# Softmax normalisation moved behind the value product in two of four attentions, with a new order of all engines' steps

## Chip, cores and metric

One core of a Trainium2 chip. The time is device microseconds of one execution; lower is better. The engines are called PE (TensorE), DVE (VectorE), ACT (ScalarE), POOL (GpSimd) and SP (the DMA queue).

## The reference

A chain of four cross attentions, a state-space layer and an MLP over x (4 batches x 1024 rows x 256, fp32); each attention has 77 keys per batch. What matters here are the third (L2) and the fourth (L3) attention, 16 heads of 16 elements each:

```
q = heads(x @ Wq + bq)                      # 16 heads of 16
s = q @ k.T / sqrt(16)                      # 77 keys, masked
p = softmax(s)                              # L2: masked again, divided by (sum + 1e-9)
o = concat over heads of p @ v              # 1024 x 256
x = x + o @ Wo + bo                         # then a layer norm
```

The second attention (L1) has 16 heads of 64, the first (L0) 8 heads of 32.

## The kernel before

**Tiling.** The 4096 rows are 32 tiles of 128 rows. Four lanes each work through 8 tiles, in two phases. The first phase (about 24 to 240 us) does L0 and the input of the state-space scan, the scan follows (to about 330 us), and the second phase does L1, L2, L3 and the MLP, for the first two batches until about 830 us and for the last two from about 890 us. Tables of keys and values are made between. Each lane owns two PSUM banks, `bank(lane, 0)` and `bank(lane, 1)`; the tiles `pr`, `front` (its part `pr2`), `big`, `zt` (the name `z` in the code), `tt` (`t`), `mx` and `rec` have one slice per lane.

**Order.** Each lane's steps stand in a list (`attention_steps`, `lane_steps`). Which lane's next step an engine takes is written out by hand, one character per step, in the strings `TURNS`, one for each engine. An engine issues its steps in this order and each step waits for semaphores, so a step that is not ready holds all that stands behind it on its engine.

**An attention of L2 or L3, in two groups of 8 heads** (`.0` in `pr`, `.1` in `front`): PE makes scores (L861), DVE adds or bounds by the mask into SBUF (L1369, L1372) and takes the row maximum (L1379), POOL subtracts (`below`, L1642), ACT takes the exponential (L1189). In L2, POOL multiplies by the mask (`maskmul`, L1628). DVE sums each head's 77 probabilities (`rowsum`, L1390), in L2 adds 1e-9 (`den_eps`, L1398), and takes 8 reciprocals per row (`recip`, L1405). The 128x616 probabilities are multiplied by them: in L2 by DVE (`weigh`, L1410), in L3 by POOL (`scale`, L1647). Then PE turns them in five 128-column pieces (`pturn`, L876), ACT and DVE copy the pieces back (`pturn_main`, L1193; `pturn_rest`, L1415), and after both groups PE multiplies by the values (`mix`, L911), with output transposed: 128 channels x 128 rows, twice. ACT copies that to SBUF (`mixed`, L1197), PE projects it (`proj`, L925) and DVE adds it to x (`resid`, L1432). L1 goes the same way with `shift` (L1385) for `below`, with `weigh`, and with no `mixed` and `proj` (its `mix` is L904). Layer norms are `stats` (L1344), `aggr` (L1348), POOL's `rstd` (L1603) and `norm` (L1357), turned by PE (`turn`, L800) and copied by ACT (L1165, L1168). POOL adds bias rows to x (`prebias`, L1616). The MLP is L961, L1213 and L972.

Of the kernel before, what the change touches and what calls it, by code (L numbers as in the profile page):

```python
# [9 lines left out]
ALU = mybir.AluOpType  # L10
# [3 lines left out]
P = 128  # L14
# [49 lines left out]
WEIGHED = (L1, L2)  # L64
# [19 lines left out]
def attention_steps(a):  # L84
# [7 lines left out]
    norm = ["rowsum"] + ["den_eps"] * (a is L2) + ["recip", "weigh" if a in WEIGHED else "scale"]  # L92
# [4 lines left out]
    steps += [(s, second) for s in masked + norm + turns] + [("mix", a.name)]  # L97
    return steps + ([] if a is L1 else [("mixed", a.name), ("proj", a.name)]) + [("resid", a.name)]
# [82 lines left out]
def setup_steps():  # L181
# [7 lines left out]
    "tensor": ("item_mm", "turn", "query", "scores", "pturn", "mix", "proj", "uproj", "ssm", "fc1", "fc2",  # L189
               "w2_mm", "wqt_mm", "k_mm", "wk_mm", "vt_mm", "vwo_mm", "v_mm", "scan_mm", "gap_turn", "more_pe"),  # L190
    "scalar": ("item_act", "turned", "query_bias", "expo", "pturn_main", "mixed", "u_sb", "gelu", "w2_sb", "wqt_sb", "k1_sb", "vt_sb", "silu", "more_act"),
    "vector": ("ctx_stats", "ctx_norm", "item_dve", "stats", "aggr", "norm", "bound", "rowmax", "shift", "rowsum", "den_eps", "recip", "weigh",
               "pturn_rest", "heads", "resid", "resume", "wk_sb", "vwo_sb", "k_sb", "v_sb", "carry", "ends", "gap", "agree"),
    "gpsimd": ("ctx_rstd", "head_masks", "row_masks", "value_zero", "zeros", "rstd", "prebias", "keep", "below", "maskmul", "scale", "gain", "offset", "masks", "fold", "vtw_zero"),
# [3 lines left out]
def lane_steps(lane):  # L198
# [12 lines left out]
    for n, run in enumerate(second):  # L211
# [19 lines left out]
        "iiiiiiii01iiiiii0iiiiiiiiiii2ii1ii230132030103132012301202103211022301321203023123021230130130032031022110101202"  # L231
        "3103212130132102013012032120132031231033012301300210302311230130321022031230132310012013201213210130230132212323"
        "1010323002103211230132130201302102332013321230030120323011012312203321203123121323231032123aa0a3aaaasaaasaasasas"
        "asaasaasaasaasaasaasaasaasaasasaasaasaasaasaasaasasasaasasasaasaasasasaaasaaaasaa0132010103123020102001010121130"
        "2100021232020130101303230301013102100002020s12011012232102111011013203030210212333213222102212013101032313203030"
        "3203312321021213203020131010030003213201320121313013212021211013032103032012023132322310221210310202313130120303"
        "3023312323120121032020131010031002303201323230131210212110132011032301312020231320322123212012032010213130301032"
        "03333231210132120302013102100300312321322131313bb2121212113bbbbb2b3bb3bb2bb3bbbb2bbbbbbbb3bbbbbb32b3bbbbbbbbbbb3"
        "bb2bbbb210221020102301002301030102130121031010333302103020210212102030312013010310030232130232103131202121102130"
        "1103203031021202313232213221021031010232313020310332330213231032101020230210013100032132102303121310131111203120"  # L240
        "2323102301202023132032213221201201301013231302030332031323231021210230201310100300123032123023103131202121120111"
        "0230320301312021302323123212201031201013231302030332330123210231212030203110130031232132323131012221321032332121"
        "32332322323332313333"),
    "vector": (
        "i0110ii013ii22i3i2iiiiiii3i0012103300123101101323330002221201101322213233200312021002012023322111213200003330322"
        "1133210101000131322301020110112221011013031222232003233301100333130223011110002001131311223220032332223033330200"
# [36 lines left out]
        "20222311113122232331322022233333233333132"),  # L283
    "sync": (
        "aaaaa2aaa0aa20a1aa3a3aaaaaa1aaaaaa102a0a13232aa020113a31a0102aa20330a1120323011a22330110322a3aa130212032a00b1aa1"
        "3312020111322300233b0bb13011012220bb2333001013301222213032302113"),
}

# [1417 lines left out]
```

## Time and profile before

| what | value |
|---|---|
| three runs | 1394.56, 1398.53, 1402.86 us (median 1398.53) |
| profiled execution | 1401.9 us, span 1400.1 us |
| mean granted TensorE clock | 0.98; 1.00 from 440 to 1280 us |
| PE busy | 1278.1 us (91%), 9411 matmuls |
| DVE busy | 1047.8 us (75%), 2236 instructions |
| ACT busy | 677.4 us (48%), 1503 instructions |
| POOL busy | 654.1 us (47%), 760 instructions |
| HBM | 23.26 MB read, 8.39 MB written |

The profile is of one execution. An instruction's duration runs from its start to the end of its writes, so a following one on the same engine may start before it ends; busy time counts each moment once. "Idle before, releaser" is the time in which an engine stood before an instruction, and the instruction that ended it. The chain is followed back from the last instruction, at each step to what released it.

### The profile page before, as it was taken

The numbers are of one execution on the slowest core, as the hardware profiler recorded it, in microseconds if no ns is written. First come the engines' busy times: TensorE is split into PE (matmuls) and PEld (weight loads), VectorE is DVE, ScalarE is ACT, GpSimd is POOL, SyncE is SP. The second block draws the span as 40 slices with busy tenths as digits, with TensorE's granted clock in tenths as the row PEclk, the third lists the DMA queues.
The fourth block names the chain that finished last, engine by engine and source line by source line (L and its number), as shares of the span: only waits on it lengthen the run. The fifth ranks groups of instructions, "written<-read, shape, count | busy, mean of one in ns | idle before, by whom it ended". The sixth has DMA issues, their size and how long they took to land.

```text
span 1400.1 us, 24568 instructions
## 1 busy us (share of the span) xinstructions
PE 1278.1 (91%) x9411; PEld 1026.3 (73%) x9411; DVE 1047.8 (75%) x2236; ACT 677.4 (48%) x1503; POOL 654.1 (47%) x760
## 2 busy tenths in 40 slices
PE   7599999959879999999999999999998999999987
PEld 5588887846667777777777787767776777777766
DVE  3478784547877888888888866888888788888863
ACT  4267766403344455545444553445544544455543
POOL 4354442012654554565555532464555555556462
PEclk9799999989999999999999999999999999999999
DMA  5523222010000000000000020000000000000000
GB/s 131 117 69 99 69 80 68 1 40 0 1 1 12 12 1 1 16 25 23 1 1 1 1 62 15 11 12 9 5 1 5 27 12 5 9 1 5 5 5 16
DMA packets 48469, 34.19 MB, mean 24 GB/s; under 512 B 22177, under 2 KB 45536, under 8 KB 48352
## 3 DMA queue, kind: packets, MB, share of 16 engines
q1 hardware_dynamic: 48304, 32.59, 8.7%
q8 instruction: 77, 1.26, 0.4%
q14 instruction: 40, 0.33, 0.1%
q10 hardware_dynamic: 48, 0.01, 0.0%
HBM read 23.26 MB, written 8.39 MB: 23 GB/s over the span
## 4 chain that ended last, share of the span: by engine, by line
PE 49%; DVE 33%; POOL 7%; SPq 4%; issue 3%; ACT 3%; DMA 1%; ACTq 0%; DVEq 0%
PE ps L876 6%; DVE mx L1379 6%; PE ps L904 5%; PE ps L925 5%; DVE mx L1390 5%; PE ps L817 4%; PE ps L851 4%; PE ps L861 4%; DVE zt L1357 3%; PE ps L972 3%; PE ps L911 3%; SPq L623 3%; DVE pr L1410 3%; PE ps L800 3%; DVE front L1410 3%
## 5 line engine op out<-in xcount | busy, mean ns | idle before, releaser
L1603 POOL TENSOR_TENSOR rstd<-mv,halfneg 128x1 f32<-128x1 f32 x192 | 109.6, 574 | 267.6 <-DVE mv L1348 266.8
L851 PE MATMUL ps<-wk,tt 128*128 128x308 f32 x512 | 148.0, 430 | 14.3 <-DVE pr L1385 14.2
L1432 DVE TENSOR_TENSOR xt<-xt,ps 128x256 f32<-128x256 f32 x160 | 66.1, 415 | 87.7 <-PE ps L925 52.1
L851 PEld LDWEIGHTS ps<-wk,tt 128*128 128x128 f32 x512 | 94.0, 192 | 48.1 <-DVE pr L1385 15.2
L1189 ACT ACTIVATE pr<-pr 128x616 f32<-128x616 f32 x128 | 90.3, 714 | 80.4 <-DVE pr L1385 44.7
L1193 ACT ACTIVATE front<-ps 128x512 f32<-128x512 f32 x96 | 57.0, 597 | 148.4 <-PE ps L876 148.4
L961 PEld LDWEIGHTS ps<-tt,fc 128*128 128x128 f32 x1024 | 117.7, 192 | 13.0 <-ACT tt L1165 9.5
L961 PE MATMUL ps<-tt,fc 128*128 128x128 f32 x1024 | 123.6, 278 | 0.9 <-ACT tt L1165 0.9
L1165 ACT ACTIVATE tt<-ps,cols 128x128 f32<-128x128 f32 x192 | 77.2, 454 | 87.2 <-PE ps L800 86.6
L1642 POOL TENSOR_TENSOR front<-mx,front 128x616 f32<-128x616 f32 x64 | 78.5, 1226 | 87.6 <-DVE mx L1379 87.4
L1357 DVE TENSOR_SCALAR zt<-xt,mv,rstd 128x256 f32<-128x256 f32 (+1 forms) x160 | 92.6, 579 | 31.7 <-POOL rstd L1603 30.6
L876 PE MATMUL ps<-ident,pr 128*128 128x128 f32 (+1 forms) x640 | 94.5, 279 | 20.7 <-DVE pr L1410 13.7
L1642 POOL TENSOR_TENSOR pr<-mx,pr 128x616 f32<-128x616 f32 x64 | 78.7, 1230 | 61.5 <-DVE mx L1379 61.1
L861 PE MATMUL ps<-kb,big 64*128 64x308 f32 x512 | 100.2, 472 | 6.4 <-ACT big L1178 2.9
L1616 POOL TENSOR_TENSOR xt<-xt,row_bo 128x256 f32<-128x256 f32 x96 | 72.7, 760 | 59.1 <-PE ps L800 29.1
L876 PEld LDWEIGHTS ps<-ident,pr 128*128 128x128 f32 (+1 forms) x640 | 71.2, 140 | 36.6 <-DVE pr L1410 22.7
L1344 DVE BATCH_NORM_STATS2 stat<-xt 128x6 f32<-128x256 f32 x192 | 80.6, 421 | 21.6 <-DMA xt<-in_x_dram 11.6
L1189 ACT ACTIVATE front<-front 128x616 f32<-128x616 f32 x96 | 67.4, 714 | 53.9 <-POOL front L1642 44.0
L1193 ACT ACTIVATE pr<-ps 128x512 f32<-128x512 f32 x128 | 75.9, 595 | 36.0 <-PE ps L876 35.6
L1379 DVE TENSOR_REDUCE mx<-ps 128x8 f32<-128x616 f32 x96 | 75.9, 792 | 22.2 <-PE ps L851 8.7
L876 PE MATMUL ps<-ident,front 128*128 128x128 f32 (+1 forms) x480 | 70.8, 279 | 14.5 <-DVE front L1410 13.8
L1390 DVE TENSOR_REDUCE mx<-pr 128x8 f32<-128x616 f32 x96 | 75.0, 782 | 10.0 <-POOL pr L1628 5.2
(219 smaller groups left out, 3087.2 us busy)
## 6 DMA issues: line engine op xcount, KB each, us to landing
out_dram<-xt SPq DMA_DIRECT2D x64, 128.0 KB, 1.8
xt<-in_x_dram SPq DMA_DIRECT2D x32, 128.0 KB, 2.7
xt<-out_dram SPq DMA_DIRECT2D x32, 128.0 KB, 2.2
fc<-in_L_xattn_fc_w_dram SPq DMA_DIRECT2D x2, 1024.0 KB, 5.6
wk<-in_L_xattn_wkv_dram SPq DMA_DIRECT2D x4, 512.0 KB, 4.9
front<-in_L_xattn_wkv_dram SPq DMA_DIRECT2D x4, 512.0 KB, 4.3
wo<-in_L_xattn_wo_dram SPq DMA_DIRECT2D x1, 1024.0 KB, 6.7
kb<-in_L_xattn_wq_dram SPq DMA_DIRECT2D x1, 1024.0 KB, 8.4
```

The source lines that it names most:

```text
L851: last = mm(bank(lane, k)[:, SFROM[k]:SFROM[k] + HB * KEYS], t[:, lane, kc, :], wk[:, kc, b, h0:h0 + HB * KEYS], start=kc == 0, stop=kc == ...
L861: last = mm(bank(lane, k)[:, SFROM[k] + n * w:SFROM[k] + (n + 1) * w], q[half, lane, c * P:(c + 1) * P], kblk[a.name][half, b, c, :, :], s ...
L876: last = turn_in(bank(lane, j // 4)[0:TROWS[j], j % 4 * P:(j % 4 + 1) * P], probs(key, lane)[:, j * P:j * P + TROWS[j]], ident[:, :])
L961: last = mm(bank(lane, c // 4)[:, c % 4 * P:(c % 4 + 1) * P], fc1[:, kc, c * P:(c + 1) * P], t[:, lane, kc, :], start=kc == 0, stop=kc == ...
L1189: ac(v, v, ACT.Exp, scale=-ATTN[key[0]].scale).then_inc(done["expo"], 1)
L1193: ac(probs(key, run.lane)[:, 0:4 * P], bank(run.lane, 0), ACT.Copy).then_inc(done["pturn_main"], 1)
L1357: v.tensor_scalar((z0 if key == "0" else z)[:, lane, own], x[:, slot(run), own], mv[:, n, 0:1], rstd[:, n:n + 1], ALU.subtract, ALU.mult). ...
L1379: v.tensor_reduce(mx[:, run.lane, group(key), :], src, AX.X, ALU.max).then_inc(done["rowmax"], 1)
L1390: v.tensor_reduce(mx[:, run.lane, group(key), :], heads_view(key, run.lane), AX.X, ALU.add).then_inc(done["rowsum"], 1)
L1410: v.tensor_tensor(p8, p8, each_head(rec, key, run.lane), ALU.mult).then_inc(done["weigh"], 1)
L1603: p.tensor_tensor(rstd[:, n:n + 1], mv[:, n, 1:2], halfneg[:, :], ALU.pow).then_inc(done["rstd"], 1)
L1642: p.tensor_tensor(p8, each_head(mx, key, run.lane), p8, ALU.subtract).then_inc(done["below"], 1)
```

## The change

In L2 and L3 the probabilities are no longer multiplied. `weigh` stays for L1 alone and `scale` goes. The row sums of both groups (16 per row) stay in `mx`. For L2 one `den_eps` over all 16 takes the place of two. One `recip` per attention writes a 128x256 tile: the reciprocal of each head's sum, 16 times over, into `z`. PE turns it in two 128-column pieces into `bank(lane, 1)` (`rturn`), ACT copies it back to `z` (`rec_t`), and DVE multiplies the transposed mix output in PSUM by it into `t` (`heads`), which was ACT's `mixed` before. `rturn` stands ahead of `mix` in each lane's list. `pturn` waits for `expo` (L3) or `maskmul` (L2) where it waited for the product; since the copies back overwrite the probabilities that `rowsum` reads, `pturn_main` and `pturn_rest` wait for `rowsum` too.

The five strings of `TURNS` are all new, in the parts of the program with no other change as well (they are left out here). The steps of PE go from 1364 to 1428, of DVE from 2199 to 2103, of POOL from 713 to 649, of ACT (1026) and SP (176) they stay. In the new order of PE, 1 to 7 of its steps lie between the second `pturn` and `rturn` of a tile, on average 3.0 in L2 and 3.3 in L3, and 1 to 4 between `rturn` and `mix`; in the new order of DVE 2 to 10 steps between the second `rowsum` and `recip` and 1 to 10 between `recip` and `heads` (mean 4.8 and 4.4).

```diff
-    norm = ["rowsum"] + ["den_eps"] * (a is L2) + ["recip", "weigh" if a in WEIGHED else "scale"]
+    norm = ["rowsum", "recip", "weigh"] if a is L1 else ["rowsum"]
...
-    steps += [(s, second) for s in masked + norm + turns] + [("mix", a.name)]
-    return steps + ([] if a is L1 else [("mixed", a.name), ("proj", a.name)]) + [("resid", a.name)]
+    steps += [(s, second) for s in masked + norm + turns]
+    if a is L1:
+        return steps + [("mix", "1"), ("resid", "1")]
+    return steps + [("den_eps", a.name)] * (a is L2) + [(s, a.name) for s in ("recip", "rturn", "rec_t", "mix", "heads", "proj", "resid")]
...
             def pturn(key, run):
-                s = "expo" if a is L0 else "weigh" if a in WEIGHED else "scale"
+                s = {"1": "weigh", "2": "maskmul"}.get(key[0], "expo")
...
+            def rturn(key, run):
+                lane = run.lane
+                pe.wait_ge(done["recip"], at("recip", key, run))
+                pe.wait_ge(done["pturn_rest"], at("pturn_rest", key + ".1", run))
+                for g in range(ATTN[key].groups):
+                    last = turn_in(bank(lane, 1)[:, g * P:(g + 1) * P], z[:, lane, g * P:(g + 1) * P], ident[:, :])
+                last.then_inc(done["rturn"], 1)
...
             def proj(key, run):
-                    pe.wait_ge(done["mixed"], at("mixed", key, run))
+                    pe.wait_ge(done["heads"], at("heads", key, run))
...
             def pturn_main(key, run):
                 act.wait_ge(done["pturn"], at("pturn", key, run))
+                if key[0] in "23":
+                    act.wait_ge(done["rowsum"], at("rowsum", key, run))
...
-            def mixed(key, run):
-                act.wait_ge(done["mix"], at("mix", key, run))
-                ac(t[:, run.lane, :, :].rearrange("p c n -> p (c n)"), bank(run.lane, 0)[:, 0:H], ACT.Copy).then_inc(done["mixed"], 1)
+            def rec_t(key, run):
+                act.wait_ge(done["rturn"], at("rturn", key, run))
+                ac(z[:, run.lane, 0:H], bank(run.lane, 1)[:, 0:H], ACT.Copy).then_inc(done["rec_t"], 1)
...
             def recip(key, run):
-                v.reciprocal(rec[:, lane, group(key), :], src).then_inc(done["recip"], 1)
+                if key[0] == "0":
+                    dst, src = rec[:, lane, 0, :], heads_out(lane)[:, :, L0.hd:L0.hd + 1].rearrange("p h o -> p (h o)")
+                elif key[0] == "1":
+                    dst, src = rec[:, lane, group(key), :], mx[:, lane, group(key), :]
+                else:
+                    dst = z[:, lane, 0:H].rearrange("p (h d) -> p h d", d=L2.hd)
+                    src = mx[:, lane, :, :].rearrange("p g h -> p (g h)").unsqueeze(2).to_broadcast([P, 2 * HG, L2.hd])
+                v.reciprocal(dst, src).then_inc(done["recip"], 1)
...
             def heads(key, run):
+                else:
+                    dve.wait_ge(done["mix"], at("mix", key, run))
+                    dve.wait_ge(done["rec_t"], at("rec_t", key, run))
+                    last = v.tensor_tensor(t[:, lane, :, :].rearrange("p c n -> p (c n)"), bank(lane, 0)[:, 0:H], z[:, lane, 0:H], ALU.mult)
...
-            def scale(key, run):
-                pool.wait_ge(done["recip"], at("recip", key, run))
-                p8 = heads_view(key, run.lane)
-                p.tensor_tensor(p8, p8, each_head(rec, key, run.lane), ALU.mult).then_inc(done["scale"], 1)
```

## Rows read from the trace of the kernel before

**Rows 1.** Windows of 440 to 800 us, second phase: busy us of each engine.
```profile
core 0: us, PE busy (x) PEld busy (x) DVE busy (x) ACT busy (x) POOL busy (x), PEclk, DMA share, GB/s
...
620.00:680.00 60.00, 56.91 (x434) 45.14 (x433) 49.46 (x101) 29.20 (x62) 32.70 (x35) 1.00 0.05 16
...
sum 360.00, PE 338.81 PEld 268.21 DVE 296.36 ACT 179.06 POOL 192.79; mean PE 56.47 PEld 44.70 DVE 49.39 ACT 29.84 POOL 32.13
```
**Rows 2.** Groups by line and shape, 440 to 800 us: tiles counted, PE's waits.
```profile
L876 PE MATMUL ps<-ident,front 128*128 128x128 f32 x140 | 21.8, 278 | 6.9 <-DVE front L1410 6.8
...
L1197 ACT ACTIVATE tt<-ps 128x256 f32<-128x256 f32 x24 | 9.2, 384 | 31.2 <-PE ps L911 31.2
```
**Rows 3.** The page's part 4: the chain that ended last.
```profile
PE 49%; DVE 33%; POOL 7%; SPq 4%; issue 3%; ACT 3%; DMA 1%; ACTq 0%; DVEq 0%
PE ps L876 6%; DVE mx L1379 6%; PE ps L904 5%; PE ps L925 5%; DVE mx L1390 5%; PE ps L817 4%; PE ps L851 4%; PE ps L861 4%; DVE zt L1357 3%; PE ps L972 3%; PE ps L911 3%; SPq L623 3%; DVE pr L1410 3%; PE ps L800 3%; DVE front L1410 3%
```
**Rows 4.** Waits: engine line <- releaser: us in total, times, longest us.
```profile
POOL front L1647 <- DVE rec L1405: 86.7, 31, 14.5
...
ACT tt L1197 <- PE ps L911: 86.1, 61, 3.4
...
DVE xt L1432 <- PE ps L925: 52.1, 41, 3.4
```
**Rows 5.** Groups by line and shape, whole span: the operations that go.
```profile
L1410 DVE TENSOR_TENSOR pr<-pr,rec 128x616 f32<-128x616 f32 x64 | 68.9, 1078 | 1.3
...
L1410 DVE TENSOR_TENSOR front<-front,rec 128x616 f32<-128x616 f32 x64 | 66.1, 1034 | 1.4
...
L1647 POOL TENSOR_TENSOR pr<-pr,rec 128x616 f32<-128x616 f32 x32 | 43.8, 1369 | 18.8 <-DVE rec L1405 18.8
...
L1647 POOL TENSOR_TENSOR front<-front,rec 128x616 f32<-128x616 f32 x32 | 39.0, 1219 | 86.7 <-DVE rec L1405 86.7
...
L1405 DVE RECIPROCAL rec<-mx 128x8 f32<-128x8 f32 x192 | 36.4, 196 | 3.8
...
L1398 DVE TENSOR_SCALAR mx<-mx 128x8 f32<-128x8 f32 x64 | 20.8, 326 | 0.7
```
**Rows 6.** Timeline of DVE: start us, us, instruction.
```profile
647.03 0.80 DVE L1385 TENSOR_TENSOR front<-mx,ps 128x616 f32<-128x616 f32 x1
647.75 0.79 DVE L1390 TENSOR_REDUCE mx<-pr 128x8 f32<-128x616 f32 x1
...
651.62 0.15 DVE L1398 TENSOR_SCALAR mx<-mx 128x8 f32<-128x8 f32 x1
651.69 0.28 DVE L1415 COPY pr<-ps 104x128 f32<-104x128 f32 x1
651.89 0.18 DVE L1405 RECIPROCAL rec<-mx 128x8 f32<-128x8 f32 x1
652.00 0.74 DVE L1390 TENSOR_REDUCE mx<-front 128x8 f32<-128x616 f32 x1
...
658.36 0.41 DVE L1432 TENSOR_TENSOR xt<-xt,ps 128x256 f32<-128x256 f32 x1
658.69 0.79 DVE L1390 TENSOR_REDUCE mx<-pr 128x8 f32<-128x616 f32 x1
```
**Rows 7.** Timeline of PE: start us, us, instruction.
```profile
661.60 0.72 PE L876 MATMUL ps<-ident,front 128*128 128x128 f32 x5
662.16 0.38 PE L800 MATMUL ps<-ident,zt 128*128 128x128 f32 x2
...
663.23 0.38 PE L800 MATMUL ps<-ident,xt 128*128 128x128 f32 x2
663.54 0.65 PE L911 MATMUL ps<-pr,vtab 128*32 128x128 f32 x16
```
**Rows 8.** Groups by line and shape, whole span: norms next to POOL.
```profile
L1357 DVE TENSOR_SCALAR zt<-xt,mv,rstd 128x256 f32<-128x256 f32 x128 | 73.7, 576 | 29.6 <-POOL rstd L1603 29.0
```

More of the change, by code:

```diff
@@ L188 @@
 MADE_BY = {
[L189 removed]
+    "tensor": ("item_mm", "turn", "query", "scores", "pturn", "rturn", "mix", "proj", "uproj", "ssm", "fc1", "fc2",
                "w2_mm", "wqt_mm", "k_mm", "wk_mm", "vt_mm", "vwo_mm", "v_mm", "scan_mm", "gap_turn", "more_pe"),
[L191 removed]
+    "scalar": ("item_act", "turned", "query_bias", "expo", "pturn_main", "rec_t", "u_sb", "gelu", "w2_sb", "wqt_sb", "k1_sb", "vt_sb", "silu", "more_act"),
     "vector": ("ctx_stats", "ctx_norm", "item_dve", "stats", "aggr", "norm", "bound", "rowmax", "shift", "rowsum", "den_eps", "recip", "weigh",
                "pturn_rest", "heads", "resid", "resume", "wk_sb", "vwo_sb", "k_sb", "v_sb", "carry", "ends", "gap", "agree"),
[L194 removed]
+    "gpsimd": ("ctx_rstd", "head_masks", "row_masks", "value_zero", "zeros", "rstd", "prebias", "keep", "below", "maskmul", "gain", "offset", "masks", "fold", "vtw_zero"),
     "sync": ("load", "put", "get", "store", "weights_get", "wkv1_get", "v0_put", "v_lay")}
@@ L235 @@
[L235 to L239, printed above, removed]
@@ L1102, in more_pe @@
                             mm(scan_out(l), ident[:, :], chunk_view(U[:, :, 1:S + 1])[:, :, :, l], start=False, stop=True).then_inc(more_mm, 1)
-            steps = {"item_mm": item_mm, "turn": turn, "query": query, "scores": scores, "pturn": pturn, "mix": mix, "proj": proj,
+            steps = {"item_mm": item_mm, "turn": turn, "query": query, "scores": scores, "pturn": pturn, "rturn": rturn, "mix": mix, "proj": proj,
                      "uproj": uproj, "ssm": ssm, "fc1": do_fc1, "fc2": do_fc2, "w2_mm": w2_mm, "wqt_mm": wqt_mm, "wk_mm": wk_mm, "k_mm": k_mm, "v_mm": v_mm,
@@ L1284, in more_act @@
                     act.sem_inc(more_r, MORE)
-            steps = {"item_act": item_act, "turned": turned, "query_bias": query_bias, "expo": expo, "pturn_main": pturn_main, "mixed": mixed, "u_sb": u_sb,
+            steps = {"item_act": item_act, "turned": turned, "query_bias": query_bias, "expo": expo, "pturn_main": pturn_main, "rec_t": rec_t, "u_sb": u_sb,
                      "gelu": gelu, "w2_sb": w2_sb, "wqt_sb": wqt_sb, "k1_sb": k1_sb, "vt_sb": vt_sb, "silu": silu, "more_act": more_act}
@@ L1395, in den_eps @@
             def den_eps(key, run):
[L1396 to L1397 removed]
+                dve.wait_ge(done["rowsum"], at("rowsum", key + ".1", run))
+                m = mx[:, run.lane, :, :]
                 v.tensor_scalar(m, m, 1e-9, None, ALU.add).then_inc(done["den_eps"], 1)
```

121 lines of the change are left out of this document (61 added, 60 removed).

## Prediction

> **What bounds the kernel now.** I read the windows first, since the change touches only the second phase. From 440 to 800 us PE is busy 338.8 of 360 us (94%), DVE 296.4 (82%), POOL 192.8 and ACT 179.1, and the granted clock is 1.00, the 2.4 GHz level, in each window [rows 1]. ACT's `mixed` ran 24 times in that stretch, two per tile [rows 2], so 12 tiles took 360 us: 30 us per tile, with 28.2 us of PE and 24.7 us of DVE. PE's missing 21.2 us are short waits; 6.8 of them stand before the turns of `front`, waiting for the weighed probabilities of DVE [rows 2]. The chain of waits says that no engine bounds alone: PE 49% of the span, DVE 33%, POOL 7%, ACT 3% [rows 3]. `weigh` stands in it with 3% for `pr` and 3% for `front` [rows 3], about 84 us of its 135.0 us busy [rows 5], so 62% of it is on the path. Over the whole chain 462 of DVE's 1047.8 busy us are on it (44%), 686 of PE's 1278.1 (54%), 98 of POOL's 654.1 (15%) and 42 of ACT's 677.4 (6%). I use these shares to turn engine time into path time. They come from a rounded page, so a term is good to about a fifth.
>
> **What goes.** (1) L2's `weigh`: 2 groups x 32 tiles = 64 of the 128 in rows 5, half of 135.0 us, 67.5 us of DVE. On the path at 0.62: 42 us. (2) L3's `scale`: 64 on POOL, 43.8 + 39.0 = 82.8 us [rows 5]. It waited for the reciprocals 105.6 us in these groups [rows 5], 86.7 of it with `front` in 31 waits [rows 4]: POOL stood ready, it isn't full. At POOL's 0.15: 12 us. Nothing behind it on POOL becomes late by its absence. (3) 128 small reciprocals. What one costs DVE's queue is its start to the next start, 651.89 to 652.00, 0.11 us [rows 6]: 14 us. Half of the `den_eps`, 10 us of 20.8 [rows 5]. Together 24 us, at DVE's 0.44: 11 us. (4) Contention. `weigh` averages 1.03 to 1.08 us [rows 5], though 616 elements with one operand in PSUM take 0.72 us start to start and 0.80 in all [rows 6]; the norms average 0.576 us [rows 8], where 256 elements need 0.41 [rows 6]. The excess is about 128 x 0.17 = 21 us for the norms, 64 x 0.26 = 17 us for the remaining `weigh` and 32 x 0.17 = 6 us for the remaining `den_eps`: 44 us. If POOL's own traffic makes it, it shrinks with POOL's load, 82.8 of 654 us, 13%: 6 us of DVE, 3 us of path. The Trainium skill (GPSIMD Engine Reference, the table of specifications) says that GpSimd shares its SBUF interfaces with VectorE, with contention for DVE instructions that have two SBUF inputs or run in a 2-port mode. By that rule the trace agrees: the slow ones are `weigh`, `norm` and `den_eps`, and a `shift` with a PSUM operand took 0.80 us [rows 6]. Sum of what goes: 42 + 12 + 11 + 3 = 68 us of path.
>
> **What comes.** (5) 64 wide reciprocals, 128x256. No row has one; its rate is the disputed price. From below, a 256-element instruction takes DVE's queue 0.33 us (658.36 to 658.69 [rows 6]). From the reciprocal's own row: 8 elements take 0.11 us, where 8 elements of `den_eps` take 0.07 (651.62 to 651.69 [rows 6]). The 616-element `shift` at 0.72 and the 256-element add at 0.33 give 0.39/360 = 1.1 ns per element, and 0.05 to 0.06 us fixed. So the reciprocal's 8 elements cost 0.05 us, 6 ns each, if its fixed part is like the others'. From above, were all 0.11 us by element, 14 ns each: 3.5 us. Between 0.33 and 3.5 us I take 256 x 6 ns + 0.06 = 1.6 us, since it goes by the only row of the operation itself, corrected by the fixed part that three other operations share; the low end would need a fixed part twice as long as theirs, the high end none. So 64 x 1.6 = 102 us of DVE.
>
> Where it lies: a wide reciprocal runs after the second `rowsum`, beside the second `pturn` and its copies, but `rturn` stands ahead of `mix` in PE's order, so what is late in it holds `mix` and all behind it. I put it on the path like the operation that it replaces in this role, 0.62: 63 us. (6) `heads`, 64 on DVE, 0.33 us each in the queue [rows 6]: 21 us. It stands between `mix` and `proj`, where ACT's copy now waits ready for PE, 86.1 us in 61 waits [rows 4], and starts at once. On DVE it may also stand behind another step of 0.7 us. Like `weigh`, 0.62: 13 us. (7) `rturn`, 128 turns on PE. A pair takes 0.31 us (663.23 to 663.54), a turn in a row of five 0.11 (0.56/5) [rows 7]; 64 pairs are 14 to 20 us, I take 16, at 0.54: 9 us. The clock is at its full level on both sides of this stretch and busier PE gives no reason for it to fall. (8) `rec_t` takes the place of `mixed` on ACT with the same shape: 0.384 us each [rows 2], no difference; it is hidden beside `mix`, which is 32 matmuls, and if it came late it would delay `heads` by at most its 0.4 us. (9) The new waits for `rowsum` in the two copies: both before and after, `rowsum` must be done before the copies can be; before, it was through `recip` and the product. If DVE is late with it, the turned groups stay in PSUM, ACT holds the exponentials behind `pturn_main`, and DVE has no copy to do itself; it is no later than it was, so nothing. (10) No DMA is added or removed; SP's 176 steps are only ordered anew, and its queues are far from full: 16 GB/s and a DMA share of 0.05 in one window [rows 1]. (11) New order in the untouched parts: same work, so a few us either way, taken as nothing. Sum of what comes: 63 + 13 + 9 = 85 us of path.
>
> **Sum.** DVE: -67.5 - 24 - 6 + 102 + 21 = +25 us, from 24.7 to about 25.5 us per tile; PE: +16 us, +0.5 per tile. POOL loses 82.8. Path: 85 - 68 = +17 us. The profiled execution took 1401.9 us (span 1400.1 and 1.8 around it) and would become 1419; it is 3.4 us above the median, so against the median of 1398.5 the forecast is 1415.5 us, 1.2% slower. The three runs spread by 0.3% to each side; 0.5% (7 us) is about what a measurement can tell from no change.
>
> **Rivals.** *Faster: the reciprocal's extra time is fixed, not by element.* One of 256 elements then takes 0.33 us more or less: 64 x 0.33 x 0.62 = 13 us in place of 63. Path: 35 - 68 = -33 us: 1365.5 us. It decides from the point where the tile costs under 1.2 us (then the sum is zero). For it: only a few hundredths of a us in rows 6 carry my rate. Against it: three other operations agree on the fixed part. It would need PE, 94% busy with 16 us more, to lose half its waits, and the removed `weigh` is behind only a third of them [rows 2]. Fully hidden reciprocals would give -46 us, 1352 us; I leave that out as an end.
>
> *No change: the reciprocal is slow, but lies in DVE's idle time*, 18% of the stretch, with POOL's freed time giving the lanes slack. At the average share of 0.44 it costs 45 us, the sum is -1 us: 1398 us. For it: it isn't on the way from exponential to turned probabilities, as `weigh` was. Against: DVE executes in order, and 1.6 us in one piece delays whatever is behind it.
>
> *Slower still: PE stands before `rturn`.* Only 1 to 7 PE steps lie between the second `pturn` and `rturn`, and 2 to 10 DVE steps between the second `rowsum` and `recip`. If an order made for short reciprocals meets long ones, PE waits in `rturn`, with `mix`, `proj` and other lanes' steps queued behind it. At 0.5 us for each of the 64 this adds 32 us: 1447 us. It decides when DVE runs more than about 3 us (three PE steps) behind PE.
>
> **How the numbers follow.** The forecast's mechanism, slow reciprocals with part on the path, 0.38 at 1406 to 1430 us; slower still, 0.15; no change, 0.17, 1392 to 1405 us; faster, 0.30, around 1365 us. The range goes from 1364 to 1446 us: it takes in the fast rival's value and nearly the slow one's, and leaves out about 0.1 on each side. Slower 0.53, same 0.17, faster 0.30. Its own range for the likeliest case is 1406 to 1430 us. Signs on both sides come from one unknown, the rate of the reciprocal.
>
> **What would show it.** RECIPROCAL 128x256 x64 at about 1.6 to 1.7 us each (0.4 in the faster rival); `weigh` x64 alone at L1410's place, with a mean near 1.0 us; POOL down by about 80 us; PE up by 14 to 20 us busy, with 128 more turns; DVE's busy share per tile near 25.5 us. The chain should name the reciprocal with about 60 us, 4%, and `weigh` with 3% in all. PE waits before `rturn` over 30 us in total would be the slower rival; DVE busier and the time unchanged the middle one. The prediction is wrong in its mechanism if the wide reciprocal takes under 1.2 us, or if it takes 1.6 us and the time still falls.

## The result and the profile after

The changed kernel takes 1362.3 us (median of 4, 1361.6 to 1367.6), the kernel before 1396.6 us beside it: ratio 0.975, 95% interval 0.972 to 0.978, 34 us faster. The forecast was 1415.5 us, slower; the measured time lies just below the range's lower end of 1364 us. The profiled execution took 1361.6 us, its span is 1359.8 us at a mean granted clock of 0.994.

The windows of the second phase after the change, with the same columns and the same stretch as [rows 1]:
```profile
620.00:680.00 60.00, 58.76 (x458) 46.73 (x457) 51.01 (x95) 30.31 (x64) 26.86 (x30) 1.00 0.00 1
...
sum 360.00, PE 341.63 PEld 275.29 DVE 294.94 ACT 179.60 POOL 158.44; mean PE 56.94 PEld 45.88 DVE 49.16 ACT 29.93 POOL 26.41
```
In 360 us, PE is 2.8 us busier, DVE 1.4 us less busy and POOL 34.4 us less busy. That is no picture of a kernel that became 34 us shorter in these steps.

The groups after, by line and shape (busy us, mean ns, idle before): those that come, and those that answer to [rows 2, 5, 8].
```profile
L1420 DVE RECIPROCAL zt<-mx 128x256 f32<-128x256 f32 x64 | 111.6, 1743 | 0.6
L1366 DVE TENSOR_SCALAR zt<-xt,mv,rstd 128x256 f32<-128x256 f32 x128 | 58.6, 460 | 33.3 <-POOL rstd L1624 32.7
L1425 DVE TENSOR_TENSOR pr<-pr,rec 128x616 f32<-128x616 f32 x32 | 30.1, 942 | 0.7
L1425 DVE TENSOR_TENSOR front<-front,rec 128x616 f32<-128x616 f32 x32 | 29.8, 932 | 0.8
L884 PE MATMUL ps<-ident,zt 128*128 128x128 f32 x128 | 27.1, 293 | 36.6 <-DVE zt L1420 36.5
L1443 DVE TENSOR_TENSOR tt<-ps,zt 128x256 f32<-128x256 f32 x64 | 26.9, 420 | 29.6 <-PE ps L918 26.5 <-ACT zt L1206 2.8
L1206 ACT ACTIVATE zt<-ps 128x256 f32<-128x256 f32 x64 | 24.5, 383 | 77.8 <-PE ps L884 77.7
L1407 DVE TENSOR_SCALAR mx<-mx 128x16 f32<-128x16 f32 x32 | 10.4, 325 | 0.0
```
The wide reciprocal (L1420) is as slow as forecast, 1.74 us. `norm` (L1366) fell from 576 to 460 ns, the remaining `weigh` (L1425) from 1.08 (`pr`) and 1.03 us (`front`) to 0.94 and 0.93 us. PE stands 36.6 us before `rturn` (L884).

The chain that ended last, after, against [rows 3]:
```profile
PE 67%; DVE 20%; issue 3%; ACT 3%; POOL 3%; DMA 2%; SPq 1%; ACTq 0%; DVEq 0%; POOLq 0%
PE ps L875 7%; PE ps L968 7%; PE ps L979 7%; PE ps L911 7%; DVE zt L1420 6%; PE ps L860 6%; PE ps L932 5%; PE ps L850 5%; PE ps L816 5%; PE ps L918 4%; PE ps L799 3%; DVE mx L1388 2%; PE ps L1075 2%; PE ps L907 2%; DVE mx L1399 2%
```
DVE's share fell from 33 to 20% although DVE is 10.8 us busier (1058.6 for 1047.8), and the strided copies of SP (L623 before, with 3%) are gone from the list. The reciprocal (L1420) stands in it with 6%, about 82 us.

**Where the 34 us lie.** I took four marks from each trace: the last write of the scan's input (the end of the first phase), the first score matmul of L1, and the last MLP matmul of the first and of the second pair of batches. "First pair" runs from the second mark to the third, "second pair" from the third to the fourth; the pairs overlap a little, and the first one's last MLP matmul is at 912.6 us before the change, later than the 830 us given above for the bulk of it. Us:

| kernel | first phase ends at | first pair takes | second pair takes |
|---|---|---|---|
| before | 233.2 | 615.8 | 484.4 |
| after | 214.3 | 595.4 | 484.4 |

The first phase has no new arithmetic, and 18.9 us are won there. The first pair of batches wins 20.4 us. The second pair does the same arithmetic as the first, new in the same places, and wins nothing (two profiles can differ by 3 us in it; see the last section). So no gain that repeats with every tile is to be seen, and I looked for single places.

Place one, the kernel before at 300 to 320 us: the window, SP's timeline (start us, us, instruction), and DVE's wait.
```profile
300.00:320.00 20.00, 5.79 (x17) 3.54 (x16) 4.45 (x10) 1.32 (x2) 2.60 (x4) 0.66 0.16 29
...
289.91 20.44 SPq L623 DMA_DIRECT2D vtab<-modrow  x24
310.39 1.48 SPq L665 DMA_DIRECT2D xt<-out_dram  x3
...
DVE xt L1438 <- DMA xt<-out_dram: 16.3, 1, 16.3
```
The same after the change:
```profile
300.00:320.00 20.00, 17.98 (x90) 12.89 (x89) 16.53 (x26) 6.92 (x15) 8.05 (x7) 0.91 0.00 1
...
271.22 10.24 SPq L622 DMA_DIRECT2D vtab<-modrow  x12
281.51 0.53 SPq L664 DMA_DIRECT2D xt<-out_dram  x1
282.16 11.01 SPq L622 DMA_DIRECT2D vtab<-modrow  x12
```
SP spends 20.44/24 = 0.85 us in issuing each strided copy into the value table. Before, lane 3's first `get` (its load of x for the second phase) stood behind all 24. DVE waited 16.3 us for it, with all lanes' steps behind that wait; PE was busy 5.8 of 20 us, and its granted clock fell to 0.66 over the window. After, all four lanes' first `get`s stand ahead of the copies.

Place two, the kernel before at 40 to 60 us: the window, SP's, POOL's and DVE's timelines.
```profile
40.00:60.00 20.00, 8.18 (x56) 7.17 (x54) 4.50 (x17) 3.66 (x7) 4.79 (x3) 0.76 0.78 143
...
35.90 10.92 SPq L623 DMA_DIRECT2D front<-wk  x12
46.86 0.52 SPq L675 DMA_DIRECT2D big<-in_mask_1x1xSxS_if_dram  x1
47.43 3.15 SPq L675 DMA_DIRECT2D out<-in_mask_BxSxS_bk_dram  x4
50.62 0.92 SPq L655 DMA_DIRECT2D xt<-in_x_dram  x1
...
55.03 0.70 POOL L1651 CAST mul<-big 128x616 f32<-128x616 int32 x1 [20.92 <-DMA out<-in_mask_BxSxS_bk_dram]
55.83 2.31 POOL L1652 TENSOR_SCALAR bound<-mul 128x616 f32<-128x616 f32 x1
58.22 2.28 POOL L1653 TENSOR_SCALAR bound<-bound 128x616 f32<-128x616 f32 x1
60.57 0.56 POOL L1603 TENSOR_TENSOR rstd<-mv,halfneg 128x1 f32<-128x1 f32 x1
...
55.31 0.43 DVE L1344 BATCH_NORM_STATS2 stat<-xt 128x6 f32<-128x256 f32 x1 [11.58 <-DMA xt<-in_x_dram]
```
Two waits stand side by side: POOL waits 20.9 us for the masks, which only L2 needs, with the second tiles' inverse deviations behind them; DVE waits 11.6 us for lane 1's second tile, whose load SP issues behind 12 other strided copies and the five mask loads. After the change that load is issued ahead of them and POOL's masks stand twelve steps later in its order:
```profile
40.00:60.00 20.00, 16.52 (x136) 14.77 (x137) 13.14 (x34) 11.41 (x31) 11.92 (x14) 1.00 0.51 59
```

### The profile page after: what moved, and what is told of

It is laid out like the page before. It is cut to its first block, busy times and chain, and to the rows that moved or that the text cites. A ratio compares the mean times of both kernels' runs of the same rounds, so it can differ in the third digit from the quotient of the medians.

```text
span 1359.8 us, 25054 instructions
## 1 busy us (share of the span) xinstructions
PE 1272.6 (94%) x9539; PEld 1036.5 (76%) x9539; DVE 1058.6 (78%) x2140; ACT 683.2 (50%) x1509; POOL 564.3 (41%) x696
## 4 chain that ended last, share of the span: by engine, by line
PE 67%; DVE 20%; issue 3%; ACT 3%; POOL 3%; DMA 2%; SPq 1%; ACTq 0%; DVEq 0%; POOLq 0%
PE ps L875 7%; PE ps L968 7%; PE ps L979 7%; PE ps L911 7%; DVE zt L1420 6%; PE ps L860 6%; PE ps L932 5%; PE ps L850 5%; PE ps L816 5%; PE ps L918 4%; PE ps L799 3%; DVE mx L1388 2%; PE ps L1075 2%; PE ps L907 2%; DVE mx L1399 2%
## 5 line engine op out<-in xcount | busy, mean ns | idle before, releaser
L1624 POOL TENSOR_TENSOR rstd<-mv,halfneg 128x1 f32<-128x1 f32 x192 | 105.5, 551 | 432.7 <-DVE mv L1357 432.4
L1420 DVE RECIPROCAL zt<-mx 128x256 f32<-128x256 f32 x64 | 111.6, 1743 | 0.6
L1366 DVE TENSOR_SCALAR zt<-xt,mv,rstd 128x256 f32<-128x256 f32 (+1 forms) x160 | 74.0, 465 | 35.7 <-POOL rstd L1624 35.1
L860 PE MATMUL ps<-kb,big 64*128 64x308 f32 x512 | 95.9, 465 | 4.2 <-DVE pr L1378 1.6
L1353 DVE BATCH_NORM_STATS2 stat<-xt 128x6 f32<-128x256 f32 x192 | 80.4, 420 | 19.7 <-POOL xt L1658 9.3
L875 PE MATMUL ps<-ident,pr 128*128 128x128 f32 (+1 forms) x640 | 91.3, 275 | 4.3 <-ACT pr L1196 1.8
L1399 DVE TENSOR_REDUCE mx<-front 128x8 f32<-128x616 f32 x96 | 75.0, 782 | 6.3 <-POOL front L1649 4.6
```

The costliest lines, as they stand in the source:

```text
L860: last = mm(bank(lane, k)[:, SFROM[k] + n * w:SFROM[k] + (n + 1) * w], q[half, lane, c * P:(c + 1) * P], kblk[a.name][half, b, c, :, :], s ...
L875: last = turn_in(bank(lane, j // 4)[0:TROWS[j], j % 4 * P:(j % 4 + 1) * P], probs(key, lane)[:, j * P:j * P + TROWS[j]], ident[:, :])
L1399: v.tensor_reduce(mx[:, run.lane, group(key), :], heads_view(key, run.lane), AX.X, ALU.add).then_inc(done["rowsum"], 1)
L1420: v.reciprocal(dst, src).then_inc(done["recip"], 1)
L1624: p.tensor_tensor(rstd[:, n:n + 1], mv[:, n, 1:2], halfneg[:, :], ALU.pow).then_inc(done["rstd"], 1)
```

## The experiments

**Order or arithmetic?** Run e1 keeps the old arithmetic and takes the new order of all engines up to the first tables; run e2 is the complement, the changed kernel with the old order up to there. One line of each of the edits, the start of SP's string:
```diff
-        "aaaaa2aaa0aa20a1aa3a3aaaaaa1aaaaaa102a0a13232aa020113a31a0102aa20330a1120323011a22330110322a3aa130212032a00b1aa1"
+        "0aaa120aaaaa3aa2aa31aaaaaaaa0011aa2332010312aaaaa23a01a20133220121003302211a30a3aaa0213213aa3211300aa2a2a00b1aa1"
```
Expected of e1: 

> The kernel before, with the changed kernel's order of all engines' steps in the setup, the first phase, the scan and the first tables, and its own order and arithmetic from the second phase on. Theory 'half of the gain is order alone': in the two profiles the last u_sb ends 18.9 us sooner (233.2 and 214.3 us) although nothing is computed otherwise there, so about 1397 - 19 = 1378 us. Rival 'the second phase's arithmetic gives all, the first phase's difference is of one execution': 1397 us, within 3.

Measured: 1382.9 us, ratio 0.990 (0.987 to 0.993), 12.6 us less, not the expected 19; first phase ends at 217.7 us, pairs 616.1 and 481.2 us.

Expected of e2: 

> The changed kernel (arithmetic and order) in the second phase, with the old order in setup, first phase and scan: the complement of e1. Theory: 1362 + 19 = 1381 us. If the two parts add, e1 and e2 lie as far below the old and above the new kernel together as the whole 34 us. Rival: 1362 us.

Measured: 1382.7 us, 0.989 (0.985 to 0.994), 12.8 us less; first phase ends at 232.2 us, pairs 596.5 and 485.3 us. By the marks the two runs split the change nearly cleanly: e1 wins 15.5 us in the first phase and nothing in the first pair, e2 1.0 and 19.3 us. By the medians 12.6 + 12.8 us are 9 us short of 34, about as much as the three intervals together allow. e2 still holds several things at once: the new arithmetic, the new order of the second phase, and SP's new order at place one.

Run e3 puts the new arithmetic into the old order, each new step where its operands are ready; the old steps keep their order on every engine (one line of the edit against after):
```diff
-        "0aaa120aaaaa3aa2aa31aaaaaaaa0011aa2332010312aaaaa23a01a20133220121003302211a30a3aaa0213213aa32113030aa2120aaa0a0"
+        "aaaaa2aaa0aa20a1aa3a3aaaaaa1aaaaaa102a0a13232aa020113a31a0102aa20330a1120323011a22330110322a3aa130212032a00b1aa1"
```

> The new arithmetic with the old order: every step that both kernels have keeps its place, and only the new steps (wide recip, den_eps, rturn, rec_t, heads) are put in between, each where its operands are ready. Theory 'arithmetic alone costs, the new order pays for it': slower than the kernel before, by the forecast's 17 us or more (the turns of the probabilities keep the late places they had behind the product): 1415 to 1450 us. Rival 'the arithmetic itself gives the second phase's 20 us': 1375 to 1385 us.

Measured: 1484.7 us, 1.062 (1.057 to 1.066), 88 us slower than before, beyond the expected 1415 to 1450 us. Both pairs are longer, 660.3 and 527.7 us. PE stands before `rturn` more than twice as long as the 36.5 us of the changed kernel:
```profile
PE ps L884 <- DVE zt L1420: 82.4, 57, 3.0
```
Put into the old order in this way, the arithmetic is a loss; it needs an order of its own. Another way of putting it in was not tried.

**SP's place.** Run e13 is the kernel before with one step of SP moved, lane 3's first `get` (the `3`) ahead of the two `v_lay` steps (`aa`); it crosses the end of one line of SP's string:
```diff
-        "aaaaa2aaa0aa20a1aa3a3aaaaaa1aaaaaa102a0a13232aa020113a31a0102aa20330a1120323011a22330110322a3aa130212032a00b1aa1"
-        "3312020111322300233b0bb13011012220bb2333001013301222213032302113"),
+        "aaaaa2aaa0aa20a1aa3a3aaaaaa1aaaaaa102a0a13232aa020113a31a0102aa20330a1120323011a22330110322a3aa130212032a00b13aa"
+        "1312020111322300233b0bb13011012220bb2333001013301222213032302113"),
```

> The kernel before, all arithmetic and all engines' orders old, but for one step of SP: lane 3's first load of x in the second phase is issued ahead of the last two tables' 48 strided copies into the value table instead of behind 24 of them. Theory (SP's order holds the first tile of lane 3 back by the 20.4 us that the 24 issues take): the first load is issued some 20 us earlier, PE is busy over 16 of 20 us in 300 to 320 us where it was 5.8, and the time falls by 14 to 20 us to 1377 to 1383 us. Rival (the lanes have slack for it, the gain is elsewhere): within 5 us of the kernel before, 1392 to 1402 us.

(The trace counts 24 copies for both tables, not the 48 of this text.) Measured: 1381.3 us, 0.988 (0.984 to 0.993). The first pair takes 596.6 us for 615.8. Window and SP's timeline of e13:
```profile
300.00:320.00 20.00, 19.73 (x93) 14.57 (x91) 16.37 (x31) 5.10 (x9) 2.47 (x4) 1.00 0.14 23
...
286.58 0.94 SPq L665 DMA_DIRECT2D xt<-out_dram  x2
289.98 20.59 SPq L623 DMA_DIRECT2D vtab<-modrow  x24
```
PE is busy 19.7 of 20 us and the clock stays at 1.00, with the 24 copies unchanged. One character is worth 15 us, and the first pair's 19.2 us are what e2 wins there too.

Run e14 is e1 with the same edit. 

> Run e1_first_new (old arithmetic, new order up to the first tables, 1382.9 us) with the same one step of SP moved. Theory (the change gains by order alone, in two separate places whose gains add): 1362 to 1370 us, the time of the changed kernel without any of its new arithmetic. Rival (the two are one gain, or the rest of it comes from the new arithmetic): 1378 to 1386 us.

Measured: 1365.6 us, 0.977 (0.973 to 0.981), against 0.975 (0.972 to 0.978) of the changed kernel: not told apart. **A gain as large as that of the change is had without its arithmetic.**

Run e16 is the changed kernel with this step moved back:
```diff
-        "0aaa120aaaaa3aa2aa31aaaaaaaa0011aa2332010312aaaaa23a01a20133220121003302211a30a3aaa0213213aa32113030aa2120aaa0a0"
+        "0aaa120aaaaa3aa2aa31aaaaaaaa0011aa2332010312aaaaa23a01a20133220121003302211a30a3aaa0213213aa3211300aa2120aaa0a30"
```

> The changed kernel with one step of SP moved back: lane 3's first load in the second phase goes behind the last two tables' 48 strided copies. Theory (that place is worth 14 to 20 us in either arithmetic): 1376 to 1384 us, or a little more since the load now waits for both tables' 21 us of issues. Rival (the new arithmetic hides it): 1360 to 1366 us.

Measured: 1384.0 us, 0.991 (0.988 to 0.994), 21.7 us above the changed kernel (here too the copies are 24, and the load is issued at 294.1 us, behind all of them). Its window of 280 to 300 us:
```profile
280.00:300.00 20.00, 2.92 (x10) 1.68 (x10) 3.42 (x10) 1.36 (x2) 2.00 (x4) 0.60 0.16 24
```

**The first phase's place.** Four runs on the kernel before. e17 moves lane 1's second load ahead of the copies (SP), e18 moves the masks ten steps back (POOL), e19 both, e20 both and the step of e13:
```diff
-        "aaaaa2aaa0aa20a1aa3a3aaaaaa1aaaaaa102a0a13232aa020113a31a0102aa20330a1120323011a22330110322a3aa130212032a00b1aa1"
+        "aaaaa2aaa0aa20a1aa3a31aaaaaaaaaaaa102a0a13232aa020113a31a0102aa20330a1120323011a22330110322a3aa130212032a00b1aa1"
...
-        "i10iiii201332a001302112233012a3201003122211033001011322102233330100011223231230000131112223332003101121032203330"
+        "i10iiii2013320013021122a33012a3201003122211033001011322102233330100011223231230000131112223332003101121032203330"
```
e17: 

> The kernel before, but for one step of SP: lane 1's second load of x, issued at 50.62 us behind the 12 strided copies of v0_put and the five mask loads, goes ahead of them. Theory (two stalls side by side: DVE stands 11.6 us before this tile's statistics, POOL stands 20.9 us before the masks, and POOL's is the longer, since its inverse deviations stand behind the masks until 60.6 us): DVE's wait on the load is gone, DVE waits for POOL instead, and the time falls by 0 to 4 us, 1393 to 1398 us. Rival (the load alone holds the stretch): 1382 to 1387 us.

Measured: 1398.4 us, 1.000 (0.998 to 1.002). The waits of e17 from 25 to 75 us:
```profile
POOL mul L1651 <- DMA out<-in_mask_BxSxS_bk_dram: 21.1, 1, 21.1
DVE fc L1357 <- POOL rstd L1603: 15.7, 1, 15.7
```
DVE's wait on the load is gone, and a wait on POOL has taken its place.

e18: 

> The kernel before, but for one step of POOL: the masks' three operations go ten steps further back, behind the inverse deviations and bias additions of the second tiles. Theory: POOL no longer holds the deviations back, but DVE still waits for lane 1's load until 55.3 us, so only the 5 us between 55 and 60.6 us are won: 1390 to 1394 us. Rival (POOL's wait alone holds the stretch): 1382 to 1387 us.

Measured: 1397.5 us, 0.999 (0.997 to 1.001): the expected 5 us did not come. The wait that stays, from the waits of e18 in the same stretch:
```profile
DVE stat L1344 <- DMA xt<-in_x_dram: 11.5, 1, 11.5
```
e19: 

> Both steps moved in the kernel before: lane 1's load ahead on SP, the masks back on POOL. Theory (the 13 us of run e1_first_new's new order are this one stall of two waits): both waits fall under 6 us, PE is busy over 14 of 20 us in 40 to 60 us where it was 8.2, 1380 to 1387 us. Rival (the first phase's gain is spread over its whole order): over 1391 us.

Measured: 1390.9 us, 0.994 (0.992 to 0.996); POOL now waits 2.1 us for the masks, DVE not at all for the load, and PE is busy 18.8 of 20 us in the window of 40 to 60 us:
```profile
40.00:60.00 20.00, 18.79 (x155) 16.99 (x153) 13.08 (x41) 13.21 (x34) 11.07 (x13) 1.00 0.80 150
```
Removing either wait alone brings nothing; removing both brings 8 us and ends the first phase 11 us earlier, at 222.2 us. That is less than the expected 12 to 19 us and just short of the rival's line of 1391 us, so part of the first phase's gain is spread over its order: the full new order ends it at 214 to 218 us, and these last 5 to 8 us I have not traced to a step.

e20: 

> Run e19_both with lane 3's first load of the second phase moved too (as in e13_get_first): three steps of the kernel before moved, none added, no arithmetic changed. Theory (the gains add, as those of e1 and e13 did in e14): 1363 to 1371 us, within 0.7% of the changed kernel's 1362.3 us. Rival (they don't add, or the first phase's gain isn't this stall): 1376 to 1384 us.

Measured: 1368.5 us, 0.979 (0.974 to 0.983). Three moved characters make 30 of the 34 us.

**The reciprocal's price.** Run e5 is the changed kernel with a reciprocal of 16 elements and a copy that spreads it, in the same order:
```diff
-                    dst = z[:, lane, 0:H].rearrange("p (h d) -> p h d", d=L2.hd)
-                    src = mx[:, lane, :, :].rearrange("p g h -> p (g h)").unsqueeze(2).to_broadcast([P, 2 * HG, L2.hd])
+                    few = rec[:, lane, :, :].rearrange("p g h -> p (g h)")
+                    short.append(lane)
+                    v.reciprocal(few, mx[:, lane, :, :].rearrange("p g h -> p (g h)")).then_inc(short_set, 1)
+                    dve.wait_ge(short_set, len(short))
+                    v.tensor_copy(z[:, lane, 0:H].rearrange("p (h d) -> p h d", d=L2.hd),
+                                  few.unsqueeze(2).to_broadcast([P, 2 * HG, L2.hd])).then_inc(done["recip"], 1)
+                    return
```

> The changed kernel, with the 128x256 reciprocal (1.66 us of the queue) replaced by one of 128x16 and a copy that spreads it over 256 (together about 0.55 us with their wait): 64 x 1.1 = 70 us less of DVE, order unchanged. Theory 'the wide reciprocal is mostly hidden, PE bounds': 0 to 10 us faster, 1352 to 1362 us. Rival, my forecast's share of 0.62 on the path: 44 us faster, 1318 us.

Measured: 1307.1 us, 0.935 (0.931 to 0.939). Its groups for the two operations, its windows' sum and its chain:
```profile
L1423 DVE COPY zt<-rec 128x256 f32<-128x256 f32 x64 | 23.2, 363 | 2.2
...
L1421 DVE RECIPROCAL rec<-mx 128x16 f32<-128x16 f32 x64 | 15.6, 243 | 0.7
...
sum 360.00, PE 356.00 PEld 289.76 DVE 279.66 ACT 180.37 POOL 158.07; mean PE 59.33 PEld 48.29 DVE 46.61 ACT 30.06 POOL 26.34
...
PE 80%; DVE 9%; ACT 3%; POOL 3%; DMA 2%; issue 2%; SPq 1%; ACTq 0%; DVEq 0%; POOLq 0%
```
111.6 - 38.8 = 72.8 us less of DVE took 55.2 us off the time, a share of 0.76. That is far from the theory's 0 to 10 us, and 11 us more than even the rival's 44. PE is busy 356 of 360 us. This is the fastest version of all, 6.5% below the kernel before and 4.0% below the changed one, and in this stretch PE bounds it alone.

Run e7 makes the wide reciprocal twice:
```diff
+                if key[0] in "23":
+                    v.reciprocal(t[:, lane, :, :].rearrange("p c (h d) -> p (c h) d", d=L2.hd), src)
```

> The changed kernel with each wide reciprocal made twice (the first into tt, unused): 64 x 1.66 = 106 us more of DVE, order unchanged. The short reciprocals of e5 took 70 us from DVE and 55 us from the time, a share of 0.78. Theory 'the wide reciprocal is on the path': at least that share, since what slack there is has been used: 83 to 106 us slower than the changed kernel, 1445 to 1468 us. Rival 'the time was saved by moving its start, not by its length': under half, below 1415 us.

Measured: 1511.9 us, 1.082 (1.078 to 1.086), 150 us above the changed kernel for 107 us of DVE (64 x 1.67), more than the theory's 83 to 106.
```profile
PE ps L884 <- DVE zt L1422: 119.1, 57, 4.0
```
This is PE's wait before `rturn` in e7 (line 1422 is the second reciprocal). It grew by 83 us, and the mean granted clock fell from 0.994 to 0.955, so part of the 150 us is PE's work at the lower clock.

**Both arithmetics with an equally good order.** For e10 (old) and e11 (new), the second phase's order was worked out anew by one procedure from the profile's durations, on the new first phase; e12 is e5 with such an order. A line of each edit, e10 against before and e11 against after:
```diff
-        "3312020111322300233b0bb13011012220bb2333001013301222213032302113"),
+        "211320011322233300011b3bb11001b0222b3332230200111133322020031123"),
...
-        "32101b132122213002b0331001bb31b1220333b2023120130032310121022133"),
+        "231011332221b13200b1023001b1bb22b1332300033322113230110210022133"),
```
e10: 

> The old arithmetic, with e1's first phase, and the order of the second phase searched anew: adjacent steps of different lanes are swapped where a replay with this case's durations, and with DVE's two-input operations and POOL's excluding each other, gets shorter. The same search and length as for e11. Theory 'order gives what arithmetic was thought to give': 1285 to 1320 us, 60 us or more below e1's 1383, and within 10 us of e11. Rival 'the new arithmetic gives the second phase's gain': over 20 us slower than e11.

e11: 

> The new arithmetic, wide reciprocals included, with the order of the second phase searched by the same method as e10. Theory 'the arithmetic is worth little either way once each has its own order': 1280 to 1315 us, within 10 us of e10. Rival: 20 us or more faster than e10.

Measured: e10 1352.9 us, 0.967 (0.964 to 0.971); e11 1321.2 us, 0.946 (0.942 to 0.949). Both miss their ranges, and at 32 us apart the rival's condition is met. But e10 still had SP's stall. Run e15 is e10 with the `get` moved as in e13. 

> Run e10_old_sum_replanned (old arithmetic, order of the second phase searched as in e11, 1352.9 us) with the same one step of SP moved. Theory: 1333 to 1339 us, so that of the 31.7 us between e10 and e11 about 17 belong to SP's order and 12 to 18 us are what the new arithmetic is worth when both have an order of their own. Rival (the new arithmetic is worth all of it): 1348 to 1356 us. Rival (it is worth nothing): 1318 to 1324 us.

Measured: 1335.8 us, 0.957 (0.951 to 0.962). First pair 580.3 us against 572.6 in e11, second 471.2 against 464.7. So the new arithmetic is worth 14.5 us once each has an order of its own and the stall is out of both. The intervals leave this about 9 us to each side, it rests on one searched order for each arithmetic, and e15's was searched with the stall still in it. Where the 14.5 us come from no run separates: DVE is busier in e11 (1051.3 us for 1008.3), PE the same (1265.8 for 1263.8), POOL less (565.3 for 650.4).

e12: 

> e5 (short reciprocal and copy) with the second phase's order searched by the same method. If PE's work bounds then, it gains little on e5's 1307: 1270 to 1295 us, and is the fastest of all. Rival 'the searched orders fit only the replay': no faster than e5.

Measured: 1310.3 us, 0.937 (0.934 to 0.940), the same as e5 (0.935); the expected 12 to 37 us did not come, and the rival's "no faster than e5" is met. The same search took 30 us off e1 (e10) and 41 us off the changed kernel (e11), so it does not fit only the replay. That it found nothing here because PE was already busy 99% of this stretch in e5 is argued, not shown.

## Why the prediction was wrong

Two steps failed, and both are about order. **Step 10** said that SP's steps are "only ordered anew, and its queues are far from full", from the DMA share of a window [rows 1]. What counted was not the queue's load but SP's own time in issuing, 0.85 us for each strided copy, and what stood behind it: worth 15 us in e13, 22 us in e16. The row that named it was shown: SPq L623 3% of the chain [rows 3]. 3% of 1400 us is 42 us, and these are three stretches of SP's timeline: the 20.4 us of place one, the 10.9 us of place two, and 10.4 us from 18.8 us on, which the change leaves as they are. I turned the shares of the four engines into factors and never asked what this one was. **Step 11** took the new order elsewhere "as nothing": it is worth 13 us in the first phase (e1), 8 of them by two moved steps (e19). Together they make up the 34 us without any new arithmetic (e14: 0.977 against 0.975).

The parts that the change does touch show the same from the other side. New arithmetic in the old order costs 88 us (e3); the new order of the second phase, with the load's place in it, then takes 102 us off (e3 to e2, 1484.7 to 1382.7 us); the new order before the second phase takes off the last 20 (e2 to the changed kernel). The sum gave the second term no place at all: it priced each operation by its average share in the old order's chain, and that is the price in neither order. The prediction's own sign of a wrong mechanism was met: the reciprocal takes over 1.6 us and the time still falls.

The steps on the arithmetic, by their numbers:

(1, 2) `weigh` and `scale` went as forecast. POOL fell by 89.8 us, 82.8 of them `scale`.

(3) `den_eps` went as forecast, half of it stays with 10.4 us. The small reciprocals fell from 36.4 to 12.8 us by their durations; the 14 us of queue time were not measured apart.

(4) Contention was undersized, and its cause was wrong. `norm` fell by 73.7 - 58.6 = 15.1 us and the remaining `weigh` by 67.5 - 59.9 = 7.6 us, 23 us where 6 were forecast for both and `den_eps`, whose mean did not change (325 ns for 326). The forecast tied the excess to POOL's load. But e15 keeps the old arithmetic with `scale`, and POOL is as busy there (650.4 us for 654.1); its order alone makes these instructions shorter still, and DVE's busy time falls by 39.5 us:
```profile
L1357 DVE TENSOR_SCALAR zt<-xt,mv,rstd 128x256 f32<-128x256 f32 x128 | 62.0, 485 | 25.4 <-POOL rstd L1603 24.9
L1410 DVE TENSOR_TENSOR pr<-pr,rec 128x616 f32<-128x616 f32 x64 | 55.9, 874 | 1.0
L1410 DVE TENSOR_TENSOR front<-front,rec 128x616 f32<-128x616 f32 x64 | 54.6, 857 | 1.1
```
What counts is which instructions the order puts side by side. How much of the 23 us is due to `scale` going and how much to the new order, the runs don't separate. It was also too quick to count `norm` and `den_eps` as agreeing with the cited rule: each has one SBUF tensor and no row shows a 2-port mode, yet the last section shows that they are stretched.

(5) Right in size, 1.67 us start to start against 1.6; the share on the path, 0.62, was low where it could be measured: 0.76 for taking 73 us away, 1.4 for adding 107 us. The chain gives the reciprocal about 82 of its 107 us, 0.76 too, where 60 were forecast. No constant share carries over such steps.

(6) `heads` has a mean of 420 ns, like the add of 256 elements (415 ns) whose 0.33 us in the queue was its price; 26.9 us goes by its durations and is no miss of the 21 us of queue time. (7) Nor are the 27.1 us of `rturn`, whose turns overlap PE's other work, to be set against the forecast 16. Set against e14, which has the same stalls gone and the old arithmetic (1268.0 us), PE's busy time grows by 4.6 us with 128 more turns, less than the forecast 14 to 20. PE waited 36.6 us before `rturn`, over the 30 us that were to mark the rival "slower still". The order also leaves it less room than I had stated: counted again, 0 to 6 steps of PE lie between the second `pturn` and `rturn`, and 1 to 9 steps of DVE between the second `rowsum` and `recip`, one fewer each. (8) `rec_t` is hidden, as forecast: DVE waited 2.8 us for it. (9) The new wait on `rowsum` shows in ACT's copies, but nothing here separates it.

In all, DVE's busy time rose by 10.8 us where the sum had +25, and the 17 us by which (4) was undersized are about this difference.

The path's sum was to be +17 us. What the runs show is that there is no single sum: +88 us in the old order (e3), about nothing when each arithmetic has the hand-made order of its own kernel and both stalls are gone (the changed kernel against e14, 3 us and within the intervals), -14.5 us when both orders are searched alike (e11 against e15). The old arithmetic in the new order was not run. e3 has the mechanism of the rival "slower still", an order made for short reciprocals that meets long ones: PE waits 82.4 us before `rturn`, and the price is larger than its 32 us. The faster rival came near the time, 1365.5 us, by luck and for a reason that is refuted: the reciprocal is not cheap. The range's lower end stood only 1.5 us under that rival's centre, though the rival had a chance of 0.30, so below it lay more than the 0.1 that was claimed.

## What to carry to other kernels

Where engines follow hand-written orders, compare the stages that the edit does not touch first: a stage that gets faster with no arithmetic changed is order alone, and moving single steps back and forth prices it. Read every releaser in the chain, SP's issuing too, for what stands behind it, and expect two waits side by side to hide each other, so that only removing both shows their price. Price an arithmetic change with an order made for it on both sides: here it was +88 us in the old arithmetic's order, about nothing between two hand-made orders, and -14 us between two searched ones.

## What the runs showed of the hardware

**The reciprocal goes by element.** 128x256 takes 1.67 us start to start (timeline of DVE, after), 6.5 ns per element; from 8 to 16 elements it grows from 201 to 243 ns, 5.3 ns each.
```profile
651.83 1.75 DVE L1420 RECIPROCAL zt<-mx 128x256 f32<-128x256 f32 x1
653.50 0.23 DVE L1432 COPY pr<-ps 104x128 f32<-104x128 f32 x1
```
**Some DVE and POOL instructions hold each other up.** DVE's and POOL's timelines, after the change:
```profile
639.17 1.81 DVE L1425 TENSOR_TENSOR pr<-pr,rec 128x616 f32<-128x616 f32 x1
...
644.80 0.80 DVE L1425 TENSOR_TENSOR front<-front,rec 128x616 f32<-128x616 f32 x1
...
639.11 1.22 POOL L1663 TENSOR_TENSOR front<-mx,front 128x616 f32<-128x616 f32 x1 [1.34 <-DVE mx L1388]
640.28 1.95 POOL L1649 TENSOR_TENSOR pr<-pr,mul 128x616 f32<-128x616 f32 x1
```
The `weigh` that starts 0.06 us after a POOL instruction takes 1.81 us and ends 0.65 us after that one does; with nothing of POOL beside it, it takes 0.80. POOL's next instruction, begun 0.70 us before this `weigh` ends, takes 1.95 us where its group's mean is 1.49. So each looks as if it stood while the other worked, for most of its time. No run isolates this, but the whole trace of the kernel before can be sorted by what runs beside the DVE instruction. "Beside it" means one of POOL's multiplies, adds or subtractions over a tile of 256 elements or more (L1616 to L1647) for more than 0.05 us. Mean ns, and how many:

| DVE instruction | nothing of POOL | such an operation beside it |
|---|---|---|
| `weigh`, 616 elements, two SBUF tensors | 795 (42) | 1218 (79) |
| `norm` into `zt`, one SBUF tensor | 410 (92) | 910 (54) |
| `den_eps`, 8 elements | 162 (29) | 522 (29) |
| `rowsum`, 616 elements | 783 (72) | 783 (113) |
| `recip`, 8 elements | 195 (101) | 198 (75) |
| `shift`, one operand in PSUM | 790 (36) | 790 (45) |

The first three are stretched, the last three are not (3 ns at most). POOL's small `rstd` (one element per row) beside `weigh` stretches nothing: 791 ns (7). For `weigh` this agrees with the Trainium skill (GPSIMD Engine Reference, the table of specifications), which names DVE instructions with two SBUF inputs. The same table names those in a 2-port mode; whether `norm` and `den_eps` are such, no run here shows. That POOL's own instruction is stretched as well is what I had not expected: `scale` takes 1217 ns on the mean with none of the three beside it (36) and 1393 with one (28).

**A stall costs clock.** The stalled windows, with PE busy 5.8 and 2.9 of 20 us, were granted 0.66 (before) and 0.60 (e16) on the mean, so part of each was at 1.2 GHz; with the stall gone it was 1.00 (e13).

**A difference with no cause in the order.** The second pair of batches has the same steps in the same order in before, e1, e13, e14 and e17 to e20. It takes 484.2 to 484.4 us in the profiles of before, e13 and e19, and 481.1 to 481.2 us in the other five. Differences of 3 us between two profiles of these kernels are not to be read.
